# A decoder layer on one core: attention maxima carried in a spare row of the queries, ScalarE's list in another order, and four whole products for TensorE

## The reference

```python
x = x + mamba(layernorm(x))           # the mixer
x = x + cross_attention(layernorm(x), ctx, ctx, mask)
x = x + mixture_of_experts(layernorm(x))   # 8 experts, the best 2 of each token
```

```python
score = where(mask == 0, -1e9, einsum('bhqd,bhkd->bhqk', qh, kh) / sqrt(8))
out = einsum('bhqk,bhkd->bhqd', softmax(score), vh)
```

## Time and profile before

| what | us |
|---|---|
| median of 3 runs | 828.37 (825.86 to 828.56) |
| the profiled execution, its own time | 829.39 |
| its span, first to last instruction | 827.6 |

### The profile page before, as it was taken

How to read it: one execution, slowest core, us unless ns; L and a number is a source line. 1 busy time by engine, 2 the same in 40 slices (tenths; PEclk the granted TensorE clock), 3 DMA queues, 4 the chain that set the end, 5 groups by cost and what they waited for, 6 DMA issues and landing times. The chain is left out here.

```text
span 827.6 us, 12373 instructions
## 1 busy us (share of the span) xinstructions
PE 686.6 (83%) x3923; PEld 479.3 (58%) x3923; DVE 684.4 (83%) x1043; ACT 523.0 (63%) x1223; POOL 618.9 (75%) x467
## 2 busy tenths in 40 slices
PE   6578667988898988889888888876679889999993
PEld 3444324556465655546555555554457678899993
DVE  3579999999999999999999999999963564765674
ACT  4677747887976878797687879567133433333345
POOL 1177988977999998999999999999771334675553
PEclk9779878999999999999999999989799999999997
DMA  4534785554648555544753663387254324787765
GB/s 106 205 116 120 211 257 176 164 176 148 190 139 223 167 167 177 181 143 128 224 165 105 193 192 118 114 224 219 69 160 155 126 97 140 249 297 235 228 240 152
DMA packets 80411, 142.70 MB, mean 172 GB/s; under 512 B 10555, under 2 KB 53574, under 8 KB 80346
## 3 DMA queue, kind: packets, MB, share of 16 engines
q1 hardware_dynamic: 75802, 133.38, 52.1%
q0 software_dynamic: 4544, 8.54, 2.9%
HBM read 110.25 MB, written 37.27 MB: 178 GB/s over the span
## 5 line engine op out<-in xcount | busy, mean ns | idle before, releaser
L1526 POOL TENSOR_TENSOR prod<-hst,BC 128x1024 f32<-128x1024 f32 x128 | 301.2, 2361 | 52.9 <-DVE hst L1741 41.8
L1741 DVE TENSOR_TENSOR_SCAN hst<-dA,Rp 128x1024 f32<-128x1024 f32 x128 | 292.3, 2283 | 9.0 <-ACT dA L1222 0.4
L1222 ACT ACTIVATE dA<-dtm,Aneg 128x255 f32<-128x255 f32 x512 | 213.9, 495 | 52.9 <-DVE hst L1741 52.1
L1531 POOL TENSOR_TENSOR prod<-prod 128x512 f32<-128x512 f32 x128 | 161.2, 1270 | 2.4
L1732 DVE TENSOR_TENSOR Rp<-BC,Rp 128x1024 f32<-128x1024 f32 x128 | 156.9, 1226 | 6.0 <-DMA BC<-bcd 0.6
L655 PE MATMUL Y<-prod,ident 128*128 128x256 f32 x512 | 140.5, 407 | 18.1 <-POOL prod L1531 14.6
L1649 POOL DMA_INDIRECT y2d<-prod,back x78 | 77.2, 989 | 97.5 <-DVE prod L2118 80.7
L655 PEld LDWEIGHTS Y<-prod,ident 128*128 128x128 f32 x512 | 101.2, 205 | 55.4 <-POOL prod L1531 20.3
L655 PE MATMUL Mb<-hpad,winT 128*128 128x512 f32 (+1 forms) x176 | 82.2, 615 | 14.7 <-ACT xh L1171 10.4
L1570 POOL DMA_INDIRECT xsd<-x2o,slots x64 | 63.1, 986 | 17.5 <-issue 16.8
L655 PEld LDWEIGHTS Rp<-BC,xh 128*128 128x128 f32 x608 | 73.6, 192 | 3.6 <-issue 1.8
(11 more groups left out here) (289 smaller groups left out, 1134.9 us busy)
## 6 DMA issues: line engine op xcount, KB each, us to landing
BC<-bcd SPq DMA_DIRECT2D x63, 1024.0 KB, 5.6
BC<-recs SPq DMA_DIRECT2D x39, 578.0 KB, 4.0
xsd<-blank SPq DMA_DIRECT2D x17, 1056.0 KB, 11.8
dtm<-xsd SPq DMA_DIRECT2D x39, 132.0 KB, 4.0
recs<-in_L_ffn_W SPq DMA_DIRECT2D x16, 256.0 KB
xin<-in_x SPq DMA_DIRECT2D x8, 256.0 KB, 5.2
x2d<-x2o SPq DMA_DIRECT2D x8, 256.0 KB, 5.6
E<-x2d SPq DMA_DIRECT2D x4, 512.0 KB, 5.4
```

The source lines that it names most:

```text
L1222: m = A(dA[:, k % RING, i, 1:SEQ], dtm[:, r % 2, d, b * SEQ + 1:(b + 1) * SEQ], ACT.Exp, scale=Aneg[:, d, c * NC + i:c * NC + i + 1])
L1526: TT(prod[:, k % RING, :, :], hst[:, k % RING, :, :], BC[:, (k // 2) % BCR, 1, :, :], ALU.mult).then_inc(s_pd, 1)
L1531: TT(prod[:, k % RING, 0:NC // 2, :], prod[:, k % RING, 0:NC // 2, :], prod[:, k % RING, NC // 2:NC, :], ALU.add).then_inc(s_fd, 1)
L1741: v.tensor_tensor_scan(hst[:, k % RING].rearrange("p n s -> p (n s)"), dA[:, k % RING].rearrange("p n s -> p (n s)"), U.rearrange("p n s - ...
```

## The change

**Maxima in a spare row.** The maxima go, unsplit and in float32, to rows of mx that stand apart: 4 of every 32 columns of 128. TensorE turns mx as it is, and ScalarE copies 32 rows each into the rows of qT that were zero for that w. The keys get a second copy: for each w they are zero in the rows of the other parity, except -1 where the maximum of their head stands. So the product of keys and queries subtracts the maximum. The mask is turned once, in round 0, and added by one product per tile.

**ScalarE's list.** The order of k = 3 to 15 changes, and decays run four ahead from k = 7 to 12, with decays(r, 10) in the slot of k = 6. On TensorE `att_variance` moves in between `conv(r+1, 1)` and `gate_in`.

**Whole products.** In steps 2, 5, 10 and 13 the fold is left out and TensorE adds all four products.

```diff
@@ tiles
-        selmax = sb("selmax", [96, HP, P], BF16)
+        twice = sb("twice", [P, 2, KEYS], BF16)
+        mbiasT = sb("mbiasT", [P, SEQ], BF16)
-        Kbd = sb("Kbd", [P, NB, HP // 2, KEYS])
+        Kbd = sb("Kbd", [P, 2, NB, HP // 2, KEYS])
-        mx = sb("mx", [P, NB * QT, HEADS])
+        mx = sb("mx", [P, NB * QT, P])
+        WHOLE = 2, 5, 10, 13
@@ TensorE
-                pe.wait_ge(s_fd, r * STEPS + k + 1)
-                for i in range(NC // 2):
+                if k in WHOLE:
+                    pe.wait_ge(s_pd, r * STEPS + k + 1)
+                else:
+                    pe.wait_ge(s_fd, folded(r, k))
+                parts = NC if k in WHOLE else NC // 2
+                for i in range(parts):
...
             def turn_max(r):
-                pe.wait_ge(Tv.sem, Tv.at("me", r))
+                pe.wait_ge(Tv.sem, Tv.at("mx3b", r))
                 for i in range(NB * QT):
-                    m = pe.transpose(Tb[0:96, i * P:(i + 1) * P], nm[:, i, :, :], identb[:, :])
+                    m = pe.transpose(T[0][:, i * P:(i + 1) * P], mx[:, i, :], ident[:, :])
...
                 for i in range(2):
                     for h in range(2):
-                        o, hp = T[h][:, i * SEQ:(i + 1) * SEQ], TRIO[g][h][i]
-                        mm(o, selmax[:, hp, :], nmT[:, b * SEQ:(b + 1) * SEQ], ...)
-                        for t in range(QT):
-                            m = mm(o[:, t * P:(t + 1) * P], mbias2[:, t, :, :], identb[:, :], ...)
+                        rows = slice(64 * h, 64 * h + 64)
+                        m = mm(T[h][:, i * SEQ:(i + 1) * SEQ], twice[rows, :, :], mbiasT[rows, :], ...)
...
                     if k == (5 if r else 6):
                         conv(r + 1, 1)
+                        if prev:
+                            att_variance(r - 1)
                         gate_in(r + 1)
-                if prev and k == 5:
+                if prev and not nxt and k == 5:
                     att_variance(r - 1)
@@ ScalarE
-                for j in range(HP // 2):
-                    m = A(Kbd[:, :, j, :], KT[:, :, :], ACT.Copy, scale=blk4[:, j:j + 1])
+                for w in range(2):
+                    for j in range(HP // 2):
+                        m = A(Kbd[:, w, :, j, :], KT[:, :, :], ACT.Identity, bias=kshift[:, w, j:j + 1], scale=kscale[:, w, j:j + 1])
...
-                A(nmT[:, :], Tb[0:96, 0:NB * SEQ], ACT.Copy).then_inc(Ta.sem, 1)
+                for w in range(2):
+                    for h in range(2):
+                        rows = slice(64 * h + 32 * (1 - w), 64 * h + 32 * (2 - w))
+                        m = A(qT[rows, w, :, :].rearrange("p b s -> p (b s)"), T[0][rows, :], ACT.Copy)
+                m.then_inc(Ta.sem, 1)
...
-                if prev and k == 5:
+                if prev and k == 3:
                     twice_contexts(r - 1)
-                if tail and k == 5:
+                if tail and k == 4:
                     att_out(r - 2)
                 if prev:
+                    if k == 4:
+                        mixer_out(r - 1)
                     if k == 5:
-                        mixer_out(r - 1)
-                    if k == 6:
                         copy_kv(r - 1)
+                        att_square(r - 1)
+                        key_blocks(r - 1)
+                if k == 6:
+                    copy_xh(r, 1)
                 if tail and k == 6:
                     spreads(r - 2)
-                if k == 6 and r < ROUNDS:
-                    copy_xh(r, 1)
                 if prev and k == 6:
-                    key_blocks(r - 1)
-                    att_square(r - 1)
+                    att_inverse_root(r - 1)
+                if k == 6:
+                    decays(r, 10)
                 if nxt and k == (6 if r else 7):
                     silus(r + 1)
-                if prev and k == 6:
-                    att_inverse_root(r - 1)
...
+                if ln and k == 14:
+                    inverse_roots_x(r + 2)
                 if prev and k == 14:
                     copy_max(r - 1)
-                if ln and k == 14:
-                    inverse_roots_x(r + 2)
-                if prev and k >= 14:
-                    exps(r - 1, 0, k - 14)
+                if nxt and k == 14:
+                    copy_xh(r + 1, 0)
+                if prev and k == 15:
+                    exps(r - 1, 0, 0)
+                    exps(r - 1, 0, 1)
...
-                g = r * STEPS + k + 3
-                if g < ROUNDS * STEPS:
+                g = r * STEPS + k + (4 if 7 <= k < 13 else 3)
+                if k != 13 and g < ROUNDS * STEPS:
                     decays(*divmod(g, STEPS))
-                if k == 15 and r + 1 < ROUNDS:
-                    copy_xh(r + 1, 0)
@@ GpSimd
                 for f in folds[k]:
-                    fold(r, f)
+                    if f not in WHOLE:
+                        fold(r, f)
@@ VectorE
-                    v.tensor_reduce(mx[:, i, h * 8:h * 8 + 8], T[h][:, :].rearrange("p (h k) -> p h k", k=KEYS), AX.X, ALU.max).then_inc(Tv.sem, 1)
-            def split_max(r):
...
+                    to = mx[:, i, 64 * h:64 * h + 64].rearrange("p (u x) -> p u x", u=2)[:, :, 0:HP // 2]
+                    v.tensor_reduce(to, T[h][:, :].rearrange("p (u j k) -> p u j k", u=2, k=KEYS), AX.X, ALU.max).then_inc(Tv.sem, 1)
...
                         maxima(r - 1, 3)
-                        split_max(r - 1)
...
+                for w in range(2):
+                    o = (1 - w) * GW
+                    nxt_(v.tensor_scalar(kscale[:, w, :], blk4[:, :], parity[:, w:w + 1], None, ALU.mult))
+                    nxt_(v.tensor_tensor(kshift[:, w, :], ident[:, o:o + HP // 2], ident[:, 64 + o:64 + o + HP // 2], ALU.add))
+                    nxt_(v.tensor_scalar(kshift[:, w, :], kshift[:, w, :], -1.0, None, ALU.mult))
```

More of the change, by code:

```diff
@@ L106, in decoder @@
         quads = sb("quads", [P, HP // 2])
+        parity = sb("parity", [P, 2])
+        kscale = sb("kscale", [P, 2, HP // 2])
+        kshift = sb("kshift", [P, 2, HP // 2])
         iota = sb("iota", [P, EXPERTS])
@@ L328, in decoder @@
         Ta = Marks(sem("Ta"), "KT V sq ln rs q m e00 e01 e10 e11 ld rd x2")
-        Tv = Marks(sem("Tv"), "xq " + " ".join(f"mx{i}a mx{i}b" for i in range(NB * QT)) + " ma mb mc md me n")
+        Tv = Marks(sem("Tv"), "xq " + " ".join(f"mx{i}a mx{i}b" for i in range(NB * QT)) + " n")
         s_kb = sem("s_kb")
+        s_mk = sem("s_mk")
         s_cT = sem("s_cT")
@@ L464, in late_half, with folded @@
             return slice(0 if r else SEQ, TOK)
+        WHOLE = 2, 5, 10, 13
+        def folded(r, k):
+            return r * (STEPS - len(WHOLE)) + sum(f not in WHOLE for f in range(k + 1))
         def step_of(k):
@@ L792, in scores @@
                         rows = slice(64 * h, 64 * h + 64)
-                        mm(T[h][:, w * SEQ:(w + 1) * SEQ], qT[rows, w, b, t * P:(t + 1) * P], Kbd[rows, b, :, :],
+                        mm(T[h][:, w * SEQ:(w + 1) * SEQ], qT[rows, 1 - w, b, t * P:(t + 1) * P], Kbd[rows, 1 - w, b, :, :],
                            start=w == 0, stop=False, skip_group_check=True)
@@ L809, in scores_t @@
                         rows = slice(64 * h, 64 * h + 64)
-                        mm(T[h][:, i * SEQ:(i + 1) * SEQ], Kbd[rows, b, 2 * g:2 * g + 2, :], qT[rows, i, b, :],
+                        mm(T[h][:, i * SEQ:(i + 1) * SEQ], Kbd[rows, i, b, 2 * g:2 * g + 2, :], qT[rows, i, b, :],
                            start=i == 0, stop=False, skip_group_check=True)
@@ L813, in scores_t @@
                     for h in range(2):
-                        o, hp = T[h][:, i * SEQ:(i + 1) * SEQ], TRIO[g][h][i]
-                        mm(o, selmax[:, hp, :], nmT[:, b * SEQ:(b + 1) * SEQ], start=False, stop=False, skip_group_check=True)
-                        for t in range(QT):
-                            m = mm(o[:, t * P:(t + 1) * P], mbias2[:, t, :, :], identb[:, :], start=False, stop=True,
-                                   skip_group_check=True)
+                        rows = slice(64 * h, 64 * h + 64)
+                        m = mm(T[h][:, i * SEQ:(i + 1) * SEQ], twice[rows, :, :], mbiasT[rows, :], start=False, stop=True,
+                               skip_group_check=True)
                 m.then_inc(Tp.sem, 1)
@@ L885, in slot @@
                         turn_contexts(k - 3)
+                    if k == 8:
+                        turn_mask()
                 if tail:
@@ L1000, in _, with turn_mask @@
             mm(T[0][:, SEQ:SEQ + 1], attT[:, 3, :], bv[:, :]).then_inc(s_tr, 1)
+            def turn_mask():
+                pe.wait_ge(s_k, 3)
+                pe.wait_ge(s_cT, 2)
+                for t in range(QT):
+                    m = pe.transpose(Tb[:, t * P:(t + 1) * P], mbias2[:, t, :, :], identb[:, :])
+                m.then_inc(s_mk, 1)
             def first_round(k):
@@ L1335, in slot @@
                         copy_contexts(k - 4)
+                    if k == 9:
```

(7 more changed lines are left out.)

37 lines of the change are left out of this document (10 added, 27 removed).

## The result

The changed kernel takes 866.3 us, the median of four runs (865.4 to 867.8); the kernel before, run beside it, 828.2. The ratio is 1.047, with a 95% interval of 1.044 to 1.049. The sign was forecast, the size was not: 846, with a range up to 858. The profiled execution took 867.1 us, with a span of 865.0.

A forecast was written before the change was run, and what follows sets the result against it. VectorE was taken to bound the rounds. 829.4 - 9.8 (split) + 26.0 (rounds 2 to 6) + 3.6 (rounds 1 and 7) - 2 (after the rounds) = 847.2, so 846 us by the median; range 830 to 858.

The forecast's parts named there:

- VectorE loses the split: VectorE's maxima: dropping five split instructions gains 1.4 us in each of seven rounds, -9.8 us.
- Scores without the selmax and mask products: scores_t saves 0.5 us per call; ScalarE's four copies of maxima cost 1.6 more, covered by some 2 us before exponentials.
- Whole products: GpSimd's saved 5.1 us a round worth nothing; TensorE's added 3.4, 1.4 after savings, hidden by idle time except in the chain.
- Rival C: TensorE becomes a bound through whole products, GpSimd waits for it and scans for GpSimd: 856 us, chance 0.10.
- First stall: VectorE's steps_x in a round waits for ScalarE's later copy_xh: 0.8 us.
- A third reader: TensorE's gates wait for the first silu, 5.5 us later; VectorE's first maxima come 3.9 us late at full clock.
- TensorE's clock: Over 5 us of idle time before the gates halves the clock: their four records take 3.4, not 1.7 us.
- Rival B: The chain holds, but the clock stays high and TensorE makes up part: 835 us, chance 0.25.
- 5.2 a round: Loss from the longer ScalarE chain in each of rounds 2 to 6, within 2.8 to 5.6: +26.0 us.
- Rounds 1 and 7: Rounds with half of the chain missing: 1.8 us lost in each, +3.6 in all.
- The start and round 0: Six small VectorE instructions added in round 0, hidden by a 1.80 us wait for ScalarE; +1 if uncovered.
- After the rounds: Experts with drained attention: dearer maxima, cheaper scores_t calls and one whole step sum to about -2 us.

The follow-up runs named there:

- e14_arranged: Changed kernel without whole products, ScalarE's list rearranged: silus to xdb close together, decays(10) and key blocks behind xdb; 829.6 us, 1.002 of the kernel before.
- e5_maxima_only: Kernel before with only the maxima in the spare row: old ScalarE list, all sixteen folds; 854.0 us, 1.034.
- e6_whole_only: Kernel before with nothing but the four whole products (twelve folds); 830.8 us, 1.003.
- e3_no_whole: Changed kernel without whole products, all sixteen folds on GpSimd; 849.6 us, 1.026 of the kernel before.
- e7: Changed kernel with the copy for steps_x and the spreads both ahead of the key blocks on ScalarE; 869.2 us, 1.051 of the kernel before.
- e16: Changed kernel with one and a half extra passes of the second convolution filling TensorE's idle time before the gates, variance product ahead of them; 856.1 us, 1.032.
- e4: Changed kernel with the copy for steps_x ahead of the key blocks on ScalarE, spreads left behind them; 870.0 us, 1.050 of the kernel before.
- e8: Changed kernel with the silus ahead of the second norm and decays(10) on ScalarE; 856.7 us, 1.037 of the kernel before.
- e2: Kernel before with nothing but the new order of ScalarE's list (TensorE's variance product moves along); 861.8 us, 1.039.
- e9: Changed kernel without whole products, ScalarE's list retuned: copy, spreads, silus, second norm, key blocks, decays(10); maxima's copies and first copy before inverse roots; 864.8 us, 1.045.
- e12: Kernel before (split, maxima apart, all folds) with ScalarE's list as in e9; 865.0 us, 1.044.
- e15: The kernel of e14_arranged with the four whole products; 831.5 us, 1.005 of the kernel before.

## Why the prediction was right in sign and wrong in size

- **VectorE loses the split: right in part.** From first scan to first scan its busy time in round 4 falls from 69.4 to 68.7 us in the changed kernel, where 1.4 less was forecast, and to 68.1 in e14_arranged. That such a gain reaches the time was wrong: with the maxima in the spare row no kernel here has a shorter round than before.
- **"Scores without the selmax and mask products", copies hidden behind some 2 us: wrong.** The duration was right (four copies 2.4 us). That the first product reads their rows was overlooked: 3.4 us more between the turn and that product, 1.8 of them without the new list. The maxima alone cost 26 us with the old list (e5_maxima_only); how that divides over this delay, the wait for the first copy and the longer key blocks was not measured.
- **Whole products "worth nothing by themselves" on GpSimd, 1.4 on TensorE in the chain: the size fails in the changed kernel.** Alone they cost 3 us in all (e6_whole_only), in it 17 (e3_no_whole). Rival C (0.10) had named TensorE, with a price of 10 us, but only half of its mechanism is there: GpSimd waits 37.2 us for TensorE in the rounds instead of 10.0, while no scan of VectorE waits for GpSimd. The products stand in TensorE's part of the loop.
- **First stall, 0.8: it was 2.34.** The keys' product came 1.5 us later in its round than in the round 6 that I had taken (it ends 24.4 us behind the first scan in rounds 2 to 4 of the changed kernel, 22.9 in mine), and the key blocks took 3.1 for 2.6 us. Round 6 was the wrong model: with 70.8 us it is shorter than rounds 2 to 4 of before, of 72.1, in which this product ends at 24.5 too.
- **The step that failed most is "A third reader", the lateness of the first maxima.** I had 3.9 at full clock and 1.7 for the clock. From first scan to first maxima it is 7.4 us later in rounds 2 to 6 on average. In rounds 2 and 3 the gates start 6.6 us later than in the same rounds before (32.8 to 39.4), not 5.5, and the first scores start 9.2 later (44.5 to 53.7), not 5.5. And the step took the chain as one that begins anew in each round, while it closes on itself: late scores make the copies of the maxima late, and with them TensorE's part of the next round.
- **"A third reader" had also left one out: there was a fourth.** The prediction priced the spreads at 2.56 as a piece of the chain, and never asked who reads their result. GpSimd does, in the middle of its list, and VectorE's `least` behind it: 2.46 us in each of six rounds. In the changed kernel this wait lies beside the loop, and e7, which shortens it to 1.83, gains nothing; it sets the round only where the silus come in time (e16).
- **TensorE's clock, 1.7 for the four records: the records are right** (3.67 for 1.98), and the 5 us of idle time before them were 6.4. What the clock costs is more in rounds 2 and 3, 2.9, since it stays low for 6.1 us there and not for the four records alone. The rule of the Trainium skill, "TensorE: Matmul & The Clock Gate", Part 1 (What's actually happening), is that activity releases a throttled clock. This run agrees: with the idle time filled, the granted clock at the gates is 1.00 (e16_filler_sized, round 5), where the changed kernel has 0.51 (round 6). Rival B, that the clock stays high, is out for the changed kernel.
- **5.2 a round "with the earlier two stalls inside it": wrong.** The stalls of one round add up to 6.3 as far as the first maxima (2.34, 2.46, 1.11, 0.19, 0.22), and 1.5 more stand at the start of round 6. Rounds 2 to 6 lost 6.2 net on average where I had 5.2 - 1.4 = 3.8: 11.9 us of the error.
- **Rounds 1 and 7, "half of the chain", 1.8 each: too little.** They lost 1.5 and 3.4 net where I had 0.4 each: 4.1 us more. Round 7 has both stalls in full. The start and round 0 came to +0.5 for 0.
- **After the rounds, -2: it was +1.1.** Two passes of eight key blocks in this stretch (1.8 more each) were left out of the sum; that these are the reason was not tried.

So the rounds account for 36.3 against 19.8 us: 11.9 + 4.1 + 0.5. The error is not one missed effect: every term of the chain was priced at its own duration, the low clock was taken as shorter than it is, and the loop was missing.

## What to carry to other kernels

When a step is moved in an engine's list, write down for every result behind it all readers on all engines, and what stands behind each reader in its own list; the price is paid there. If the round closes on itself, look for the loop first, by going back from wait to wait: taking away the visible stalls (e4, e7) moved them, and only what lies in the loop (e3, e8, e16) shortened the round. Work taken off the busiest engine is a gain only if the loop has room; here up to 1.3 us a round less of VectorE's work were never seen in the time.

## What the runs showed of the hardware that I had not expected

- Useless matmuls made a kernel faster: 5.2 us of them a round, in idle time, took 10 us off 866, since the four records behind them ran in 1.98 instead of 3.4 to 3.8 us, and in two rounds those after them faster too.
- The length of the idle time alone does not tell the clock behind it. After 3.62 us idle in round 5 of e8_silus_early the gates ran at full clock (1.98); after the same 3.62 us in round 2 of that run they took 3.37, with a granted clock of 0.57. After 2.48 us idle in round 4 of the kernel before two records of 128 columns took 0.80 us, where at full clock two take 0.39:

```profile
335.76 0.80 PE L655 MATMUL T<-attT,oT 128*128 128x128 f32 x2 [2.48 <-DVE oT L1779]
```

- Rounds of very different lists took the same time: 75.1 to 75.5 us in most rounds of e2, e3, e8 and e16, 78.2 to 78.5 in most rounds of e7, e9, e12 and the changed kernel, 71.9 in most of e14 and e15. The low clock explains the step from 75.4 to 78.3 between e16 and rounds 2 and 3 of the changed kernel; the others are not explained.
- On ScalarE a copy of 128x128 with a scale takes 386 ns, and with a bias as well (Identity) 482; started one behind the other 0.32 and 0.385 apart.
